# Attention's negated row maxima: the bf16 value and its rest made on GpSimd instead of VectorE

## The reference, cut to what matters

```python
q, k, v = proj(Wq, bq), proj(Wk, bk), proj(Wv, bv)        # (2, 16, 2048, 8)
scores = einsum('bhqd,bhkd->bhqk', qc, k) * scale          # for chunks of queries
scores = where(k_pos > q_pos, -inf, scores)
m = max(scores, axis=-1, keepdims=True)
p = softmax(scores - m, axis=-1)
out = einsum('bhqk,bhkd->bhqd', p, v)
```

## Time and profile before

| what | value |
|---|---|
| median of three runs | 1975.16 us (1974.81 to 1977.96) |
| the profiled execution, its own time | 1976.67 us |
| its span, first to last instruction | 1975.0 us |
| attention, from the first score product to the last | about 76 to 945 us |
| mean granted TensorE clock | 0.921 of full speed |

### The profile page before, as it was taken

How to read it: one execution, slowest core, us unless ns; L and a number is a source line. 1 busy time by engine, 2 the same in 40 slices (tenths; PEclk the granted TensorE clock), 3 DMA queues, 4 the chain that set the end, 5 groups by cost and what they waited for, 6 DMA issues and landing times. The chain is left out here.

```text
span 1975.0 us, 42847 instructions
## 1 busy us (share of the span) xinstructions
PE 1624.5 (82%) x14150; PEld 1057.9 (54%) x14150; DVE 1423.3 (72%) x2559; ACT 952.3 (48%) x2093; POOL 688.7 (35%) x498
## 2 busy tenths in 40 slices
PE   4599989998998998999646648999999999976183
PEld 3233333333333333333435548888889888875173
DVE  6789988888988888987331246888888888874222
ACT  4177777777777776777421122333333333332020
POOL 5400000000000000000144326877777777853632
PEclk9699999999999999999857878999999999996597
DMA  3200000000000000000162151222222222204423
GB/s 115 83 18 19 18 15 16 18 19 20 19 19 12 18 19 20 19 18 2 70 217 73 44 147 35 86 76 79 79 85 78 80 76 85 85 22 147 153 68 104
DMA packets 171647, 117.12 MB, mean 59 GB/s; under 512 B 10940, under 2 KB 161852, under 8 KB 171208
## 3 DMA queue, kind: packets, MB, share of 16 engines
q1 hardware_dynamic: 167368, 106.33, 18.2%
q0 software_dynamic: 4096, 8.46, 1.2%
HBM read 63.98 MB, written 50.72 MB: 58 GB/s over the span
## 5 line engine op out<-in xcount | busy, mean ns | idle before, releaser
L562 DVE TENSOR_REDUCE chunk_max<-ps_max 128x1 f32<-128x512 f32 (+3 forms) x1280 | 703.8, 603 | 103.1 <-PE ps_max L667 56.6
L611 ACT ACTIVATE probs<-ps_s 128x512 f32<-128x512 f32 (+3 forms) x1280 | 612.6, 536 | 215.0 <-PE ps_s L659 106.5
L640 PE MATMUL ps_s<-Qs,Ks 50*128 50x512 bf16 (+3 forms) x1280 | 368.0, 353 | 37.9 <-DVE chunk_max L562 22.0
L650 PE MATMUL ps_max<-Ks,Qs 48*128 48x512 bf16 (+3 forms) x1280 | 377.3, 360 | 13.2 <-POOL a_ident L504 10.6
L712 PE MATMUL ps_o<-probs,Vp 128*32 128x512 f32 (+3 forms) x2560 | 343.9, 562 | 5.2 <-ACT O_sb L594 4.8
L1424 POOL TENSOR_TENSOR lane_products<-L,q 128x1024 f32<-128x1024 f32 x132 | 309.4, 2374 | 3.9 <-DMA L<-scanned 3.9
L519 POOL TENSOR_TENSOR A_b<-A_newton,b_tile 128x128 f32<-128x128 f32 x32 | 14.6, 457 | 811.3 <-ACT A_newton L614 811.3
L640 PEld LDWEIGHTS ps_s<-Qs,Ks 50*128 50x128 bf16 x1280 | 98.4, 93 | 370.0 <-DVE chunk_max L562 313.6
L1479 DVE TENSOR_TENSOR weighted<-exp_scores,psV_s 128x4096 f32<-128x4096 f32 x44 | 194.2, 4413 | 0.2 <-issue 0.2
L1437 POOL TENSOR_TENSOR q<-L,z_normed 128x1024 f32<-128x1024 f32 x44 | 141.5, 3216 | 144.5 <-DVE z_normed L1459 144.5
L1558 PE MATMUL psS<-ident,lane_products 128*128 128x128 f32 x1408 | 169.2, 279 | 23.9 <-POOL lane_products L1424 23.9
(11 more groups left out here) (224 smaller groups left out, 2317.8 us busy)
## 6 DMA issues: line engine op xcount, KB each, us to landing
scanned<-q SPq DMA_DIRECT2D x44, 512.0 KB
L<-scanned SPq DMA_DIRECT2D x44, 512.0 KB
m_w<-in_L_ffn_w_dram SPq DMA_DIRECT2D x32, 512.0 KB
Qs<-q_parts SPq DMA_DIRECT2D x192, 32.0 KB
Ks<-k_parts SPq DMA_DIRECT2D x192, 32.0 KB
dispatched<-m_blank SPq DMA_DIRECT2D x2, 2080.0 KB
m_blank<-dispatched SPq DMA_DIRECT2D x16, 260.0 KB
routed<-m_blank SPq DMA_DIRECT2D x2, 2048.0 KB
```

Source lines behind the costliest of these rows:

```text
L562: nc.vector.tensor_reduce(out, scores[:, 0:w], axis=AX.X, op=ALU.max).then_inc(max_reduced, 1)
L611: nc.scalar.activation(dst, ps_s[(k + r) % R][:, q0:], ACT.Exp, scale=SCALE).then_inc(exp_done, 1)
L640: last = nc.tensor.matmul(ps_s[(k + r) % R][:, q0:], K[r][rows, kt * P:(kt + 1) * P], Q[r][rows, g * QW + q0:(g + 1) * QW], start=True, st ...
L650: last = nc.tensor.matmul(ps_max[(k + r) % R][:, 0:w], Q[r][rows, i * P:(i + 1) * P], K[r][rows, ck * QW:ck * QW + w], start=True, stop=no ...
```

## The change

`negate_maxima` keeps only its reduction (L532). Two GpSimd instructions, `split_maxima`, take the place of the other two: an add of a tile of zeros (`no_max`) that writes the bf16 value, and the same subtraction as before. GpSimd waits for VectorE's reduction, and between its own two instructions for the first of them. `turn_rows` now waits for GpSimd. In a section GpSimd runs both halves of the next head behind its Newton steps. One more tile is set to zero at the start.

```diff
-    FILLED, MADE = 2 * R + 2, 3 * R + 3
+    FILLED, MADE = 2 * R + 3, 3 * R + 4
+        no_max = sb("no_max", [P, NQ // 2])
-        neg_max_steps = sem("neg_max_steps")
+        neg_max_done, neg_max_split = sem("neg_max_done"), sem("neg_max_split")
-            for t, value in [... (probs0, 0.0), (ones_row, 1.0)]:
+            for t, value in [... (probs0, 0.0), (ones_row, 1.0), (no_max, 0.0)]:
@@ gpsimd
+            def split_maxima(s, r, f):
+                half = neg_max_b[r][:, f]
+                pool.wait_ge(neg_max_done, s * 2 + (f + 1))
+                nc.gpsimd.tensor_tensor(half[:, 0, :], neg_max[r][:, f, :], no_max[:], ALU.add).then_inc(neg_max_split, 1)
+                pool.wait_ge(neg_max_split, s * 4 + (2 * f + 1))
+                nc.gpsimd.tensor_tensor(half[:, 1, :], neg_max[r][:, f, :], half[:, 0, :], ALU.subtract)\
+                  .then_inc(neg_max_split, 1)
             def section(s, j, r, p, exp, nxt):
...
+                if nxt:
+                    for f in range(2):
+                        split_maxima(s + 1, (r + 1) % R, f)
@@ vector
             def negate_maxima(s, r, f):
-                half = neg_max_b[r][:, f]
                 nc.vector.tensor_reduce(neg_max[r][:, f, :], chunk_max[r][:, f * NQ // 2:(f + 1) * NQ // 2, :],
-                                        axis=AX.X, op=ALU.max, negate=True).then_inc(neg_max_steps, 1)
-                dve.wait_ge(neg_max_steps, s * 6 + (3 * f + 1))
-                nc.vector.tensor_copy(half[:, 0, :], neg_max[r][:, f, :]).then_inc(neg_max_steps, 1)
-                dve.wait_ge(neg_max_steps, s * 6 + (3 * f + 2))
-                nc.vector.tensor_tensor(half[:, 1, :], neg_max[r][:, f, :], half[:, 0, :], ALU.subtract)\
-                  .then_inc(neg_max_steps, 1)
+                                        axis=AX.X, op=ALU.max, negate=True).then_inc(neg_max_done, 1)
@@ tensor
-                pe.wait_ge(neg_max_steps, s * 6 + 3 * (f + 1))
+                pe.wait_ge(neg_max_split, s * 4 + 2 * (f + 1))
```

More of the change, by code:

```diff
@@ L496, in _ @@
             n = 0
-            for t, value in [(t, 0.0) for t in Vp] + [(t, LEAST) for t in chunk_max] + [(probs0, 0.0), (ones_row, 1.0)]:
+            for t, value in [(t, 0.0) for t in Vp] + [(t, LEAST) for t in chunk_max] + [(probs0, 0.0), (ones_row, 1.0), (no_max, 0.0)]:
                 nc.gpsimd.memset(t[:], value).then_inc(made, 1)
```

## The result

| | before | after |
|---|---|---|
| median of 19 runs each, us | 1977.14 (1974.45 to 1980.66) | 1979.63 (1977.05 to 1983.37) |
| profiled execution: span, us | 1975.0 | 1977.2 |
| VectorE busy, us (share) | 1423.3 (72%) | 1399.9 (71%) |
| GpSimd busy, us (share) | 688.7 (35%) | 715.5 (36%) |

The ratio is 1.0015, with a 95% interval of 1.0008 to 1.0022: slower by 3.0 us, 1.6 to 4.3 (the two medians lie 2.5 us apart). VectorE has 23.4 us less to do, and the kernel takes longer. The median of before is 2 us above that of the three runs from which the prediction started.

The account below looks back on a forecast made before the run. It took the bound to be waits between engines, with half 1's transpose on the path and VectorE's work there having slack. 6.2 - 2.1 + 0.1 = +4.2 us on 1975.16 gave 1979.4 us, range 1972.4 to 1985.0.

Parts of the forecast that it names:

- The path at half 1: Between two heads, VectorE's reduction through transpose, products, step 3, exponential, copy to step 7: transpose 0.23 us later, not absorbed.
- GpSimd's instruction at 0.24 us: Each of the two new GpSimd instructions on 128x8 takes 0.24 us, making half 1's path 0.69 us instead of 0.46.
- the longer line: Line through GpSimd's two-input rows of 128 and 4096 elements, giving 205 ns at 8 elements.
- the nearer pair: GpSimd's two-input rows of 128 and 512 elements, whose line gives 239 ns at 8 elements; the forecast used it.
- 27 heads: Heads where TensorE waits for the split at half 1, each losing 0.23 us: +6.2 us.
- Half 0 worth nothing: After reduction 11, VectorE's 0.41 us gains nothing, because reduction 13 waits for TensorE's product of step 13.
- Section -1 gives 2.1 us: At the start, reduction 12 no longer waits for the L535 that took 1.85 us beside GpSimd's bias add: -2.1 us.
- The zero tile at 0.1 us: One memset ahead of the first product costs 0.11 us.
- VectorE is the bound: Rival, 3%: VectorE gets back 0.41 us twice a head in 26 plain heads, 23.3 us in all, giving 1951.9 us.
- the transpose is not on the path: Rival, 7%: something else sets step 3 and step 7, so only section -1 counts, 1973.2 us.
- a cheap instruction, under 0.16 us: Rival, 12%: GpSimd's instruction costs 0.112 us like a memset, 1972.4 us; below 0.16 us the kernel is not slower.
- a dear one, over 0.3: Rival, 25%: GpSimd's instruction costs 0.34 us, giving 1984.8 us, or 0.457 us, giving 1991.0 us.

Follow-up runs that it names:

- third_pool_step: The changed kernel with one more GpSimd add, and its wait, in the chain of half 1: plain head 26.578 us, 1.0051 of before.
- half0_pool_c: Against the kernel before, only half 0 split on GpSimd, same semaphore and wait values, VectorE's additional wait behind reduction 12: plain head 26.151 us, ratio 0.9997.
- dve_dummies_b: The changed kernel with VectorE also doing a copy and subtraction nobody reads, without a wait behind the subtraction: plain head 26.298 us, 1.0011 of before.
- Before_no_bias: The kernel before without GpSimd's bias add (L508): L535 of section -1 took 0.17 us instead of 1.85, and section -1 22.0 us instead of 23.7.
- after_again: The changed kernel once more, unaltered, for a second trace: plain head 26.293 us, end of section -1 at 99.10 us.
- after_turn_late: The changed kernel with step 2's products issued ahead of the transpose of half 1: plain head 25.789 us, 0.9952 of before.

## Why the prediction was right, point by point

It had 1979.4 us (1972.4 to 1985.0) and 0.42 for no change within 0.2%, 0.53 for slower. The median came at 1979.63 us. That closeness is mostly luck, since before's median rose by 2 us with the larger set. The move itself is +3.0 us (1.6 to 4.3) against +4.2: right in its sign, but within the 0.2%, which the prediction held for the less likely of the two. Its own terms, with what they measured, give 3.9 - 2.1 = +1.8 us.

- *The path at half 1*: right. Each link of it moved by the same 0.15 us, and third_pool_step shows that a delay there counts in full.
- *GpSimd's instruction at 0.24 us*: the term that was mis-sized. It took 0.20, what the longer line gave (0.205) and not the nearer pair. The hand-overs measured 0.07, 0.08 and 0.05 us, as taken. The transpose came 0.60 us after the reduction and not 0.69, so the delay was 0.14 and not 0.23.
- *27 heads*: right for 26 of them; 26 x 0.15 = 3.9 us against 6.2. TensorE waited for GpSimd's subtraction 27 times, the 26 and the last head; in the four heads over the loop's end it came late by itself, as assumed.
- *Half 0 worth nothing*: right, by the 0.42 us of idling, by half0_pool_c and by dve_dummies_b.
- *Section -1 gives 2.1 us*: right, 2.06. Before_no_bias shows the cause of 1.7 of them.
- *The zero tile at 0.1 us*: the memset took 0.09 us, but the first weight load of the scores came at 76.65 us, against 76.66 before. It cost nothing.
- *What it did not have*: section 0 became 1.3 us shorter and the loop's ends 1.55 us longer. They nearly cancel. The first goes with the clock: the granted clock of the stretch from 104 to 106 us was 0.50 before, which is the lower of TensorE's two levels (1.2 GHz), and 1.00 after (2.4 GHz).

```profile
104.00:106.00 2.00, 2.00 (x11) 0.20 (x8) 1.53 (x3) 1.18 (x3) 0.00 (x0) 0.50 0.06 21
```
```profile
104.00:106.00 2.00, 2.00 (x33) 1.16 (x30) 1.59 (x3) 1.62 (x5) 0.29 (x1) 1.00 0.33 98
```

(Columns: stretch and length, busy us of PE, PEld, DVE, ACT and POOL with counts, granted clock, share and GB/s of the DMAs; before, then after.) Before, the rise came about 4 us later while the section had only begun 2.1 us later. In half0_pool_c section -1 ended as late as before (101.20), but the clock of the stretch from 106 to 108 us was 1.00 and not 0.52, and section 0 took 26.42 us. So the 1.3 us goes with the moment at which the clock rose, and the change is not shown to have set that moment.

The loop's ends go with the clock too, which falls to the lower level after the turn, where TensorE has stood for about 3 us (before, it was busy for 0.99 of the 4.00 us from 284.4, at a granted clock of 1.00). In a stretch of 8 us that holds all of the lower clock, the mean granted clock and the length of the head were:

| kernel | 1st turn | 2nd | 3rd | 4th |
|---|---|---|---|---|
| before | 0.79, 30.04 us | 0.79, 30.20 | 0.79, 30.34 | 0.57, 31.23 |
| after | 0.57, 31.18 | 0.79, 30.49 | 0.57, 31.00 | 0.79, 30.69 |
| after_again | 0.57, 31.37 | 0.79, 30.18 | 0.57, 31.12 | 0.79, 30.37 |
| after_turn_late | 0.57, 31.77 | 0.57, 31.60 | 0.57, 31.62 | 0.57, 31.56 |

A turn with 0.57 is 0.5 to 1.0 us longer than one with 0.79 in the same trace; the changed kernel had two of them, before one, and after_turn_late four, so up to 3 us of the 4.7 that it gave back there (its waiting for issue, 13.6 us against 12.1, is another 1.5). Why a turn gets the one or the other is open. TensorE's own waiting for issue at the turns grew from 12.1 us to 12.9,

```profile
PE ps_s L646 <- issue: 12.9, 4, 3.4
```

but it was 12.2 us in after_again, whose four heads were 1.2 us longer than before all the same.

- *The rivals*: "VectorE is the bound" falls with dve_dummies_b; "the transpose is not on the path" with third_pool_step; a cheap instruction, under 0.16 us, and a dear one, over 0.3, with the 0.20 measured. The clock did not fall in a plain head, even with the longer wait of third_pool_step (1.00). The Trainium skill (GPSIMD Engine Reference, section 3, Performance versus the Vector engine) gives a ratio of 1.96 between the engines at 2048 elements; at 8 elements the ratio here was 0.199 / 0.166 = 1.2, so that ratio should not be carried down to short operands.

## What to carry to other kernels

Ask of a freed engine what it waits for right behind the freed place; if it is another engine, and stays so after the change, its time is worth nothing, and a chain handed to a second engine costs its hand-overs in full where someone stands waiting for it. Here the same TensorE queue held a microsecond of work that did not need the result: issued first, it covered either split, and was worth more than twice what moving the instructions cost. And a kernel made to undo half of a change needs its waits in the same places with the same values, or it measures its own sequencer steps.

## What the runs showed of the hardware that I had not expected

- A GpSimd add or subtraction of 128x8 takes 0.20 us, with 0.07 us from VectorE and 0.28 us from one dependent step to the next; VectorE's takes 0.17 and 0.21.
- A 0.17 us cast on VectorE took 1.85 us beside a long two-input GpSimd instruction and ended with it. The reductions beside the same instruction, whose input is in PSUM, kept their pace (eight in 4.07 us beside it, in 4.08 without it), and so did the negation, whose input is in SBUF (0.19 us at 83.45). The Trainium skill (SBUF — State Buffer, Who interferes with whom) has a cast on VectorE able to hold or wait for a port pair that it shares with GpSimd, for the whole instruction, and reductions never; the traces agree.
- A wait for a value long reached, counted by a register, cost VectorE 0.11 us on the path (0.33 to 0.44), and TensorE's queue with two semaphores in place of one started a block of products 0.10 us later (0.15 us behind the copy and not 0.05).
- At the loop's turns the granted clock fell to its lower level every time, and for longer in some turns than in others (0.79 or 0.57 over 8 us), which made the head 0.5 to 1.0 us longer.
